# Summing the sixteen slices of a bilinear layer: a strided sum against three additions of contiguous halves

## What is computed

```python
node = h @ W1                                   # (4096,16)
hw = jnp.einsum('nc,kcf->nkf', h, W2)           # (4096,16,128)
x = jnp.einsum('nk,nkf->nf', node, hw)          # sum over k of node[n,k] * hw[n,k,:]
x = adj @ x
x = x + node @ b
return jax.nn.relu(x)
```

## Time and profile before

| | us |
|---|---|
| median of 3 runs | 2235.76 |
| lowest, highest of them | 2234.46, 2236.96 |
| the profiled execution, its own time | 2233.43 |
| span of the profiled execution | 2231.6 |

### The profile page before, as it was taken

How to read it: one execution, slowest core, us unless ns; L and a number is a source line. 1 busy time by engine, 2 the same in 40 slices (tenths; PEclk the granted TensorE clock), 3 DMA queues, 4 the chain that set the end, 5 groups by cost and what they waited for, 6 DMA issues and landing times.

```text
span 2231.6 us, 30437 instructions
## 1 busy us (share of the span) xinstructions
PE 1819.9 (82%) x8958; PEld 871.5 (39%) x9101; DVE 1693.7 (76%) x1792; ACT 1398.4 (63%) x1767; POOL 188.7 (8%) x154
## 2 busy tenths in 40 slices
PE   4221573899999999999797799999986699986997
PEld 4111221344444444444345344444452244462332
DVE  4555327788898888889466788888859988846998
ACT  1676006788788788788234567676645577625886
POOL 0000001100000000000442000000017700000000
PEclk7555788899999999999897899999979999977999
DMA  5997025555555554554500311221030089713542
GB/s 160 430 427 312 0 79 209 166 153 160 157 153 156 166 153 149 169 154 155 208 0 0 78 38 38 60 54 38 1 133 0 0 348 428 314 38 78 96 92 76
DMA packets 79540, 313.86 MB, mean 141 GB/s; under 512 B 13942, under 2 KB 14422, under 8 KB 69462
## 3 DMA queue, kind: packets, MB, share of 16 engines
q1 hardware_dynamic: 79468, 312.98, 41.7%
HBM read 297.88 MB, written 15.08 MB: 140 GB/s over the span
## 4 chain that ended last, share of the span: by engine, by line
PE 40%; DVE 10%; POOL 3%; issue 3%; ACT 1%; DMA 1%; DVEq 0%; SPq 0%; POOLq 0%; ACTq 0%; another core or an unknown queue 0%
PE psum L925 8%; PE psum L915 8%; PE psum L988 7%; PE psum L859 7%; POOL halves L484 3%; DVE hidp L1363 2%; DVE xT L1385 2%; DVE yT L1382 2%; DVE prod L1422 2%; PE psum L883 1%; PE psum L885 1%; PE psum L726 1%; PE psum L731 1%; PE psum L897 1%; PE psum L737 1%
## 5 line engine op out<-in xcount | busy, mean ns | idle before, releaser
L586 ACT ACTIVATE ss<-KR,dpt 128x1024 bf16<-128x1024 int16 x384 | 413.1, 1138 | 112.0 <-DVE pl L1255 111.3
L859 PE MATMUL psum<-ph,Tt 128*128 128x512 bf16 x1502 | 412.2, 381 | 8.8 <-DVE pl L1255 7.0
L669 ACT ACTIVATE hid<-psum,fB 128x512 f32<-128x512 f32 x416 | 270.7, 686 | 143.7 <-PE psum L915 89.0
L925 PE MATMUL psum<-hidp,fW 128*128 128x512 bf16 x1218 | 291.7, 381 | 28.6 <-DVE hidp L1363 22.6
L915 PE MATMUL psum<-hTp,fW 128*128 (+1 forms) x1229 | 291.3, 381 | 4.5 <-ACT mk L654 3.2
L1363 DVE TENSOR_TENSOR hidp<-hid,hidp 128x512 bf16<-128x512 f32 x416 | 268.7, 687 | 25.9 <-DVE xT L1385 10.1
L1252 DVE TENSOR_TENSOR ph<-ss,Ahi 128x3072 bf16<-128x3072 bf16 x128 | 225.2, 1759 | 62.0 <-PE psum L859 60.3
L859 PE MATMUL psum<-pl,Tt 128*128 128x512 bf16 x752 | 226.0, 381 | 0.8
L859 PEld LDWEIGHTS psum<-ph,Tt 128*128 128x128 bf16 x1536 | 150.3, 98 | 190.6 <-issue 6.4
L1255 DVE TENSOR_TENSOR pl<-ss,Alo 128x3072 bf16<-128x3072 bf16 x128 | 224.1, 1751 | 0.0
L925 PEld LDWEIGHTS psum<-hidp,fW 128*128 128x128 bf16 x1248 | 117.4, 98 | 190.2 <-issue 49.9
(11 more groups left out here) (228 smaller groups left out, 2111.0 us busy)
## 6 DMA issues: line engine op xcount, KB each, us to landing
Ar<-in_adjT SPq DMA_DIRECT2D x32, 2048.0 KB, 12.9
Ab<-in_adjT SPq DMA_DIRECT2D x128, 512.0 KB, 4.2
A<-in_adjT SPq DMA_DIRECT2D x32, 2048.0 KB, 10.4
Tt<-T_d SPq DMA_DIRECT2D x128, 256.0 KB, 2.6
mB<-mk_d SPq DMA_DIRECT2D x128, 256.0 KB, 8.0
T_d<-tb SPq DMA_DIRECT2D x32, 256.0 KB, 2.0
RD<-rden_d SPq DMA_DIRECT2D x12, 512.0 KB, 5.4
fWs<-in_W SPq DMA_DIRECT2D x2, 2304.0 KB, 16.8
```

Of the source, the lines that this page charges most:

```text
L586: last = nc.scalar.activation(ss[s % 2][:, h, :], KR[:, h, rb * RB:(rb + 1) * RB], ACT.Sigmoid, scale=STEP, bias=dpt[:, ds(t * HEADS + h, 1)])
L669: nc.scalar.activation(hid[j % HB][:, :], psum[:, j % HB, :], func, bias=fB1[:, j:j + 1]).then_inc(act_done[k], 1)
L859: last = nc.tensor.matmul(psum[:, 2 * h + q, :], Tt[s % AS][:, h, w, :], mv[:, q * CH:(q + 1) * CH], start=fresh and k == 0, stop=False, s ...
L925: last = nc.tensor.matmul(psum[:, HB + e % dn, :], fW[1][x][:, j * P:(j + 1) * P], hidp[j % ring][:, y, :], start=(f == 0 and w == 0), sto ...
```

## The change

The eight rows in `halves[s]` are no longer summed by one strided `tensor_reduce`. Three `tensor_tensor` additions of contiguous halves do it: 512 columns onto 512 in place, 256 onto 256 in place, and 128 plus 128 into `xf[s]`; each of the first two is linked to the next. The cast to bf16 moves from VectorE to ScalarE (`high_x`), the subtraction `split_x` from GpSimd to VectorE. `products` now runs two slices ahead of the slice that is split and one ahead of the one that is summed. GpSimd keeps `halve` alone. PE, the scaling and the sizes of all buffers stay.

```diff
@@ GpSimd
             pool.sem_inc(b_half, 2)
-            pool.sem_inc(b_x, 2)
-            halve(0, 0)
-            with pool.Fori(0, NT // 2 - 1) as i:
+            with pool.Fori(0, NT // 2) as i:
                 for s in range(2):
-                    halve(2 * i + s + 1, 1 - s)
-                    split_x(2 * i + s, s)
-            halve(NT - 1, 1)
-            split_x(NT - 2, 0)
-            split_x(NT - 1, 1)
+                    halve(2 * i + s, s)
@@ ScalarE
+            def high_x(n, s):
+                act.wait_ge(b_sum, n + 3)
+                nc.scalar.activation(Xb[0][:, ds(n, 1), :].rearrange("p o f -> p (o f)"), xf[s][:, :],
+                                     ACT.Copy).then_inc(b_x_hi, 1)
+
+            scaled_products(0, 0)
+            scaled_products(1, 1)
+            with act.Fori(0, NT // 2 - 1) as i:
                 for s in range(2):
...
+                    scaled_products(2 * i + s + 2, s)
+                    high_x(2 * i + s, s)
+            high_x(NT - 2, 0)
+            high_x(NT - 1, 1)
@@ VectorE
             def summed(n, s):
+                bc = Chain(dve, dve_steps, chained + 2 * n)
                 dve.wait_ge(b_half, n + 3)
-                dve.wait_ge(b_x, n + 1)
-                V.tensor_reduce(xf[s][:, :], halves[s][:, :, :].rearrange("p k f -> p f k"), AX,
-                                ALU.add).then_inc(b_sum, 1)
-                dve.wait_ge(b_sum, n + 3)
-                V.tensor_copy(Xb[0][:, ds(n, 1), :].rearrange("p o f -> p (o f)"), xf[s][:, :]).then_inc(b_x_hi, 1)
-
+                bc.link(V.tensor_tensor(halves[s][:, 0:4, :], halves[s][:, 0:4, :], halves[s][:, 4:8, :], ALU.add))
+                bc.link(V.tensor_tensor(halves[s][:, 0:2, :], halves[s][:, 0:2, :], halves[s][:, 2:4, :], ALU.add))
+                V.tensor_tensor(xf[s][:, :], halves[s][:, 0, :], halves[s][:, 1, :], ALU.add).then_inc(b_sum, 1)
+
+            def split_x(n, s):
+                dve.wait_ge(b_x_hi, n + 1)
+                V.tensor_tensor(Xb[1][:, ds(n, 1), :].rearrange("p o f -> p (o f)"), xf[s][:, :],
+                                Xb[0][:, ds(n, 1), :].rearrange("p o f -> p (o f)"), ALU.subtract).then_inc(b_x, 1)
...
             products(0, 0)
+            products(1, 1)
+            summed(0, 0)
             with dve.Fori(0, NT // 2 - 1) as i:
                 for s in range(2):
-                    products(2 * i + s + 1, 1 - s)
-                    summed(2 * i + s, s)
-            products(NT - 1, 1)
-            summed(NT - 2, 0)
+                    products(2 * i + s + 2, s)
+                    summed(2 * i + s + 1, 1 - s)
+                    split_x(2 * i + s, s)
             summed(NT - 1, 1)
+            split_x(NT - 2, 0)
+            split_x(NT - 1, 1)
```

More of the change, by code:

```diff
@@ L691, in _, with scaled_products @@
             act.sem_inc(b_prod_a, 2)
-            with act.Fori(0, NT // 2) as i:
-                for s in range(2):
[L694 to L701, removed]
+            def scaled_products(n, s):
+                act.wait_ge(b_ps, n + 1)
+                act.wait_ge(b_half, n + 1)
+                for k in range(K1 // 2):
+                    last = nc.scalar.activation(
+                        prod[s][:, k, :], psum[:, 4 * s + k // 4, k % 4 * P:k % 4 * P + P], ACT.Copy,
+                        scale=nodek[:, ds(n, 1), k:k + 1].rearrange("p o k -> p (o k)"))
+                last.then_inc(b_prod_a, 1)
+            def high_x(n, s):
[5 more added lines that the diff above has]
+            with act.Fori(0, NT // 2 - 1) as i:
+                for s in range(2):
+                    scaled_products(2 * i + s + 2, s)
+                    high_x(2 * i + s, s)
+            high_x(NT - 2, 0)
+            high_x(NT - 1, 1)
             act.wait_ge(b_x, NT + 2)
@@ L1427, in summed @@
             def summed(n, s):
+                bc = Chain(dve, dve_steps, chained + 2 * n)
                 dve.wait_ge(b_half, n + 3)
-                dve.wait_ge(b_x, n + 1)
-                V.tensor_reduce(xf[s][:, :], halves[s][:, :, :].rearrange("p k f -> p f k"), AX,
-                                ALU.add).then_inc(b_sum, 1)
-                dve.wait_ge(b_sum, n + 3)
-                V.tensor_copy(Xb[0][:, ds(n, 1), :].rearrange("p o f -> p (o f)"), xf[s][:, :]).then_inc(b_x_hi, 1)
+                bc.link(V.tensor_tensor(halves[s][:, 0:4, :], halves[s][:, 0:4, :], halves[s][:, 4:8, :], ALU.add))
[5 more added lines that the diff above has]
+                                Xb[0][:, ds(n, 1), :].rearrange("p o f -> p (o f)"), ALU.subtract).then_inc(b_x, 1)
+            chained = c.n
+            dve.sem_inc(b_x, 2)
             products(0, 0)
+            products(1, 1)
+            summed(0, 0)
             with dve.Fori(0, NT // 2 - 1) as i:
                 for s in range(2):
-                    products(2 * i + s + 1, 1 - s)
-                    summed(2 * i + s, s)
-            products(NT - 1, 1)
-            summed(NT - 2, 0)
+                    products(2 * i + s + 2, s)
+                    summed(2 * i + s + 1, 1 - s)
+                    split_x(2 * i + s, s)
             summed(NT - 1, 1)
+            split_x(NT - 2, 0)
+            split_x(NT - 1, 1)
+            c.n += 2 * NT
             dve.wait_ge(b_node, 2)
```

## The result

The changed kernel takes 2268.22 us (median of 4 runs, 2268.01 to 2269.49) against 2235.11 us for the kernel before (4 runs, 2232.58 to 2236.96) on the same chip: a ratio of 1.0154, 95% interval 1.0137 to 1.0170. It is 33 us slower. The prediction said 2266 us, within 2254 to 2281.

A forecast was written before the change was run, and what follows sets the result against it. The prediction took `halve` on GpSimd and `products` on VectorE, tied by the held cast, as the bound. Periods 28.1, start 0.6 and drain 1.2 sum to 29.9 us more: 2263.3 profiled, 2266 us median, range 2254 to 2281.

The forecast's parts named there:

- What bounds the kernel: Bilinear stage: `halve` and `products` alternate, VectorE's cast being held until `halve` ends; 3.81 us a slice.
- Which kind the additions are: VectorE's additions, with two SBUF inputs, take turns with GpSimd operations that read SBUF; the reduction does not.
- A1: First of the three VectorE additions, 128x512, 0.69 us; expected to get its turn before `halve`.
- A2: Second VectorE addition, 128x256, 0.425 us alone; expected to be held behind `halve` and recorded at 2.4 to 2.5 us.
- the 5.2 us order: Slice order with `halve` taking the first turn, ahead of A1: period 5.2 us, 12 us more in all; 6%.
- The period: One slice of the changed stage: 4.78 us against 3.81, which is 28.1 us over 29 slices.
- the loop's branch: VectorE's loop cost between subtraction and `products`: 0 to 0.1 us every second slice, left unpriced.
- Start and drain: Ends of the stage: `products` of slice 2 starts 0.6 us late, and the end after the last `products` takes 1.2 more.
- Rival 1: In the slice loop the additions run beside `halve`: some 2.8 us a slice, 29 us less, 2206 us; 6%.
- Rival 2: VectorE keeps the ports through all additions and the subtraction: 3.87 us a slice, 2239 us, up to 2254 if mixed; 7%.
- Rival 3: TensorE falls to the slow 1.2 GHz clock: period some 5.25 us, 14 us more, 2280 us; 6%.
- What costs nothing: ScalarE's cast (0.38 us a slice), GpSimd's lost subtraction (0.43 us) and TensorE's matmuls were said not to change the time.

The follow-up runs named there:

- cast_alone: Kernel before with the cast moved to ScalarE and `products` two slices ahead; reduction stays on VectorE, subtraction on GpSimd: 2212.9 us, ratio 0.9905.
- moves_alone: Changed kernel with the additions undone, one strided reduction again; cast on ScalarE, subtraction on VectorE: 2236.1 us, ratio 1.0008 to the kernel before.
- unrolled: Changed kernel with VectorE's slice loop written out six slices to a turn instead of two: 2267.1 us, ratio 1.0147 to the kernel before.
- adds_alone: Kernel before with only the reduction replaced by the three additions; cast stays on VectorE, subtraction on GpSimd: 2276.6 us, ratio 1.0191.
- write_only: Changed kernel with `halve` replaced by a GpSimd constant fill that reads nothing from SBUF; result not computed: 2204.5 us, one run.
- later_turn: Changed kernel with GpSimd's `halve` waiting for the sum of the slice before instead of two before: 2242.1 us, ratio 1.0037 to the kernel before.

## Why the prediction was right, point by point

**What bounds the kernel.** Right, and tested from both sides: with the cast gone from VectorE the slice falls from 3.81 to 3.07 us (cast_alone), with the subtraction held in its place it stays (3.86, moves_alone). Between those two kernels only the subtraction's engine and its order differ.

**Which kind the additions are.** Right. Every count of time behind the other engine came out as the earlier trace rows gave it: `halve` ended 2.22 us after A1 (2.21 reckoned), A2 0.28 us after `halve` (0.28). A1 got the first turn in all 32 slices (none of its records is over 0.69 us), as chosen, not `halve` (the 5.2 us order).

**The period.** The steps gave 4.78 us; the slices without a branch took 4.75 to 4.76. The slices with a branch took 5.08 to 5.10. Over both 4.91. *The term that was mis-sized is the loop's branch*: put at 0 to 0.1 us every second slice and taken as nothing in the sum, measured at 0.33. Over the 14 slices that have it that is 4.6 us. The prediction gives no reason for its small value, and the slices of before, all 3.80 to 3.83 us, could not show the price: there the branch comes behind the cast, recorded at 0.67 us with its hold. unrolled shows it in the changed kernel. What hides it is not the hold as such but how long VectorE's last instruction before it takes: behind the subtraction of 0.28 us it costs 0.33, behind adds_alone's cast of 0.23 us 0.38; behind the held cast (0.67), the held subtraction (0.96) and cast_alone's reduction (1.93, not held) nothing.

**Start and drain.** 0.6 and 1.2 us reckoned, 0.8 and 1.0 measured. **The sum.** 29.9 us reckoned, 33.8 in the stage: 4.6 more from the branch and 0.7 less from periods a little shorter (4.755 us for 4.78). That the number came so near, 2268.2 for 2266, owes a little to luck. Between the medians the change is 33.1 us, and the 29.9 was added to a median of before (2235.76) that later came out 0.65 lower. The two profiled executions differ by more, 2269.49 - 2233.43 = 36.1 us (29.9 reckoned), of which 1.7 lie ahead of the stage, in when the first `products` begins.

**One sign was misread.** The prediction wanted `halve` recorded at 2.7 to 2.8 us. Its own steps, issue at 0.22 and end at 2.82, give 2.60, and 2.58 to 2.59 was measured.

**The rivals.** Rival 1 (beside each other) was excluded by A2's record (2.46 us), and write_only shows what it would have given. Rival 2 (VectorE keeps its turn through all additions) does not happen: a gap of 0.04 us between A1 and A2 was enough for GpSimd. later_turn makes it happen by a wait, and gives 2242 us, within what was given for it. Rival 3 (the clock) happened in part. The windows of the changed kernel (length, busy us of PE, PEld, DVE, ACT, POOL, PEclk) against the earlier trace rows:

```profile
1700.00:1740.00 40.00, 26.77 (x95) 9.82 (x97) 38.44 (x41) 20.14 (x75) 20.69 (x8) 0.86 0.00 0
```

and TensorE's timeline in it:

```profile
1710.99 2.76 PE L967 MATMUL psum<-bw,h3b 128*128 128x512 bf16 x12 [0.64 <-DVE prod L1423]
1716.32 2.54 PE L967 MATMUL psum<-bw,h3b 128*128 128x512 bf16 x11 [2.56 <-DVE prod L1423]
1720.85 4.45 PE L967 MATMUL psum<-bw,h3b 128*128 128x512 bf16 x12 [1.99 <-DVE prod L1423]
```

Some groups of twelve matmuls ran in part at the slow pace, 4.45 us instead of 2.76. The granted clock from 1720.8 to 1725.4 was 0.63, so part of that group ran at the 1.2 GHz level. It came after a pause of 1.99 us. The group before it came after a pause of 2.56 us and had 1.00, the 2.4 GHz level, so the pause alone doesn't tell. Over the 40 us the mean was 0.86, where the kernel before had 1.00. No cost of it can be seen: from slice 3 on none was longer than 5.10 us, and those all 5.08 to 5.10 or 4.75 to 4.76, whatever the pace of their matmuls. The prediction's cover, one slice's time, was enough, where rival 3 took it to be used up. In cast_alone, where TensorE pauses 0.2 to 0.7 us, the clock of the stretch was 1.00 again.

**What costs nothing.** Right for the cast on ScalarE (0.31 us, with 58.5 us of idle time in front of it). That GpSimd's lost subtraction gains nothing was not tested by itself; it fits the 86.3 us for which `halve` waits.

## What to carry to other kernels

Before an operation is replaced by a faster one, look in the trace for its kind beside a GpSimd operation that reads SBUF. Three additions that take 1.4 us alone cost more here than a reduction of 1.93 us that runs beside GpSimd, because A1 keeps `halve` waiting and A2 then waits for `halve`. The number of inputs in SBUF is a hint and not the whole test: the additions have two and are held, the reduction has one and is not, but the cast has one too and was held (0.67 us for 0.23). No run here tells the cast and the reduction apart. An operation recorded several times longer than its size warrants, and ending 0.1 to 0.3 us behind one of GpSimd's, is being held; move that one to ScalarE, as the cast of 0.23 us here, which with the longer lead of `products` was worth 21 us. And a cost that a trace doesn't show may be one that a long instruction or a stall covers: when that goes or moves, it appears (the branch, 0.33 us).

## What the runs showed of the hardware

- VectorE and GpSimd do not meet only at semaphores, as was said at the start: they also exclude each other in SBUF. In the changed kernel the turn passed at the end of each instruction to the one that waited, though the same engine's next one was 0.04 us away: A2 was held in 31 slices, A1 in none. A held operation ends its own length less some 0.14 us after the other: 0.28 for 256 columns, 0.15 for 128 (moves_alone), 2.22 for GpSimd's 1024.
- A GpSimd fill of 128x1024 f32 took 0.95 us, and neither held nor was held by VectorE additions (write_only).
- The reduction from 1024 elements to 128, read with a stride, took 1.93 us; `products`, also 1024 elements a partition, took 1.22. No run here tells whether the stride or the reduction makes that difference. Still it was the better choice.
- A loop's branch on VectorE cost 0.33 us a turn behind an instruction of 0.28 us (0.38 behind one of 0.23), and nothing behind one of 0.67, 0.96 or 1.93 us, held or not.
